# Second layer's self-attention: fourteen matmuls that nothing reads, in every step, at three places of TensorE's order

## The reference

```python
# x: (16, 128, 256); N_Q, N_KV = 16, 4 heads of 16; g = 4
q = _rope((x @ Wq + bq) by heads)          # 16 query heads
k = _rope((x @ Wk + bk) by heads)          # 4 key heads
v = (x @ Wv + bv) by heads                 # 4 value heads
qg = q.reshape(B, N_KV, g, T, d)
scores = einsum('bhgnd,bhsd->bhns', qg, k) / sqrt(d)   # the 4 queries of a group are summed
att = softmax(where(tril, scores, -inf))
y = einsum('bhns,bhsd->bhnd', att, v)      # width 4 * 16 = 64
x = x + (y @ Wo + bo)                      # x on the right went through a layer norm first
```

## Time and profile before

| | us |
|---|---|
| median of 3 runs | 3545.29 (3538.87 to 3551.51) |
| profiled execution, its own time | 3557.57 |
| span of its profile | 3555.8 |
| mean granted TensorE clock | 0.925 of full speed |
| TensorE busy | 2974.0 (84% of the span) |
| VectorE, ScalarE, GpSimd busy | 2398.8, 1808.0, 1772.2 |

### The profile page before, as it was taken

The page is one execution under the profiler, slowest core; times in us unless marked ns, Lnnn a source line. Parts: engine busy times, 40 slices in busy tenths (PEclk is TensorE's granted clock), DMA queues, the critical chain, the costliest instruction groups (busy, mean ns, idle before and its releaser), DMA issues. The chain is left out here.

```text
span 3555.8 us, 73082 instructions
## 1 busy us (share of the span) xinstructions
PE 2974.0 (84%) x25401; PEld 2294.0 (65%) x25432; DVE 2398.8 (67%) x5594; ACT 1808.0 (51%) x3484; POOL 1772.2 (50%) x1923
## 2 busy tenths in 40 slices
PE   8959978779998664976768998999998777877798
PEld 5747754457777453654556665888886666666565
DVE  5567744747777416857867887566665777776788
ACT  3347743446665223645653332566664565665476
POOL 2122211215555374547744851788885666665232
PEclk9979998689998776988998999999999999999799
DMA  4010010000001251000014000000000000000001
GB/s 148 1 23 13 15 62 6 1 5 8 7 7 51 93 114 41 6 22 13 16 24 172 19 18 8 2 0 0 0 0 6 4 5 4 3 4 3 22 24 38
DMA packets 92844, 89.37 MB, mean 25 GB/s; under 512 B 41279, under 2 KB 83167, under 8 KB 91234
## 3 DMA queue, kind: packets, MB, share of 16 engines
q1 hardware_dynamic: 88034, 81.23, 7.4%
q0 software_dynamic: 4608, 5.57, 0.9%
HBM read 68.16 MB, written 11.53 MB: 22 GB/s over the span
## 5 line engine op out<-in xcount | busy, mean ns | idle before, releaser
L518 PE MATMUL bank<-l2f_xnT,l2f_wi 128*88 128x512 f16 x960 | 222.1, 381 | 1.0 <-DVE l2f_h L364 0.7
L1527 PE MATMUL bank<-l3a_ln_xnT,far 128*128 128x128 f16 x3072 | 185.8, 221 | 1.8 <-POOL l3a_ln_xnT L1343 1.8
L2319 ACT ACTIVATE l3x_prob<-bank,l3x_less,l3x_q_rr 128x128 f32<-128x128 f32 x256 | 96.5, 457 | 171.8 <-DVE l3x_less L2201 171.8
L1527 PEld LDWEIGHTS bank<-l3a_ln_xnT,far 128*128 128x128 f16 x3072 | 180.9, 99 | 3.4 <-POOL l3a_ln_xnT L1343 2.2
L518 PEld LDWEIGHTS bank<-l2f_xnT,l2f_wi 128*88 128x88 f16 x960 | 114.7, 121 | 80.8 <-issue 2.4
L377 DVE SCALAR_TENSOR_TENSOR x_res<-bank,l3f_combine,x_res 128x256 f32<-128x256 f32 x320 | 132.8, 478 | 25.0 <-PE bank L528 23.0
L377 DVE SCALAR_TENSOR_TENSOR x_res<-bank,l2f_combine,x_res 128x256 f32<-128x256 f32 x320 | 132.5, 476 | 6.9
L2793 PE MATMUL bank<-l0x_v,l0x_pT 128*128 128x128 f32 x1024 | 134.5, 279 | 3.2 <-ACT l0x_pT L3208 1.5
L2793 PEld LDWEIGHTS bank<-l0x_v,l0x_pT 128*128 128x128 f32 x1024 | 127.6, 192 | 13.8 <-issue 4.7
L528 PE MATMUL bank<-l3f_wd,l3f_h 128*128 128x256 f16 x960 | 119.0, 274 | 12.4 <-DVE l3f_h L369 12.4
L2407 POOL TENSOR_TENSOR l1x_prob<-l1x_prob,l1x_srec 128x512 f32<-128x512 f32 x64 | 67.9, 1061 | 121.8 <-DVE l1x_srec L2178 121.8
(11 more groups left out here) (717 smaller groups left out, 9556.1 us busy)
## 6 DMA issues: line engine op xcount, KB each, us to landing
far<-in_l1f_in SPq DMA_DIRECT2D x32, 256.0 KB, 3.4
sums<-near SPq DMA_DIRECT2D x2, 2176.0 KB, 19.0
far<-in_l1f_down SPq DMA_DIRECT2D x32, 128.0 KB, 3.5
l1f_xn<-sums SPq DMA_DIRECT2D x32, 128.0 KB, 2.3
l2f_wi<-in_l2f_in SPq DMA_DIRECT2D x20, 176.0 KB
far<-l0x_kT SPq DMA_DIRECT2D x64, 48.0 KB
far<-l2x_kT SPq DMA_DIRECT2D x32, 96.0 KB
l3f_wi<-in_l3f_in SPq DMA_DIRECT2D x20, 128.0 KB
```

The lines of the kernel that those rows point to most:

```text
L518: last = nc.tensor.matmul(bank[g % 2][0:width, :], wi16[u][p][:, a, k, :], xnT[q][:, k, 512 * g:512 * g + 512], start=(k + p + q == 0), st ...
L1527: last = nc.tensor.matmul(bank[:, P * j:P * j + P], w(k, 512 * c + P * j, P, p), norm.xnT[u][q][:, k, :], start=(k + p + q == 0), stop=(k ...
L2319: last = nc.scalar.activation(prob[c_ % 2][:, at], b_s[:, at], ACT.Exp, bias=less[c_ % 2][:, j:j + 1], scale=q_rr[c_ % 2][:, j:j + 1])
```

## The change

A helper `keep_busy(g, n)` is added to TensorE's list and called three times a step. For the kind `"summed"` and a sequence number `g` of 1 or more it does `n` matmuls of 256 columns with the first weight half of the output projection as both operands (64 rows), into columns 0 to 255 of the score bank that is free in this step. Nothing reads what they write, they wait for nothing and signal nothing. The next `scores` into that bank overwrite it. It is called with 2 between `scores` and `scores_by_key`, with 6 between `turn_k` and `turn_q`, and with 6 between `turn_norm` and `turn_out`: 14 a step, in the 15 steps with sequences 1 to 15, so 210 in all. For the other layers and for sequence 0 it does nothing.

```diff
+                def keep_busy(g, n):
+                    if kind == "summed" and g:
+                        for _ in range(n):
+                            nc.tensor.matmul(b_s[(g + 1) % 2][:, 0:D], w16["o"][0][0:FW, 0, 0:P], w16["o"][0][0:FW, 0, :],
+                                             start=True, stop=True)
+
                 def turn_k(b):
...
                     for u in range(min(2, UB)):
                         if new is not None:
                             scores(new, u)
+                    keep_busy(new, 2)
                     for u in range(min(2, UB)):
                         if back is not None:
                             scores_by_key(back, u)
                     if kt is not None:
                         turn_k(kt)
+                    keep_busy(new, 6)
                     if tn is not None:
                         turn_q(tn)
                     if pj is not None:
                         if ctxT is not None:
                             project_ctx(pj)
                         turn_norm(pj)
+                    keep_busy(new, 6)
                     for u in range(UB):
                         if fin is not None and u == UB // 2:
                             turn_out(fin)
```

## The result

The changed kernel takes 3541.36 us (median of 20, 3537.15 to 3543.50), the kernel before, run beside it, 3554.99 us (median of 20, 3535.06 to 3558.62; the three executions that the forecast started from are among them). The medians lie 13.6 us apart. The ratio over all executions, which gives the few short ones of the kernel before their weight, is 0.9974, 95% interval 0.9963 to 0.9984: faster by 0.26%, less than the 0.43% that was forecast, and just inside the 0.3% that I had named as the border. A second comparison, further down, gave 0.9965 (0.9952 to 0.9977). The forecast of 3530 us was too low by 11; the measured median lies 0.6 us inside the upper end of its range of 3522 to 3542.

What follows compares the result with a forecast made beforehand. TensorE's chain, two thirds of it at half clock because of two waits for ScalarE, was taken as the bound. Full steps -20.4 and ends +5.2 gave -15.2 us off the 3545.3 median: 3530 us, range 3522 to 3542.

Steps and rivals of the forecast that it cites:

- What bounds the kernel, and why the clock would hold: Eighth-slice layer, TensorE's chain at mean clock 0.67; filling its waits leaves 0.4 of 7.6 us idle, holding the upper clock.
- clock holds as reckoned: Likeliest case: upper clock kept through the layer's full steps, kernel at 3530 us; chance 0.67.
- The step at the upper clock: Full steps: 7.36 us from start-to-start pieces, 7.59 with the added 0.23; eight take 60.7 instead of 81.07, -20.4 us.
- first place: Two matmuls between scores and scores_by_key, where nothing waits: 0.23 us a step on the path.
- The ends: Sequences 1, 2 and 11 to 15, where added work is partly uncovered: +1.9, +0.9 and +2.4, together +5.2 us.
- The base: Whole kernel: the -15.2 us reckoned from the 3557.57 us profile, taken off the median 3545.3, giving 3530 us.
- in part: Rival: in the full steps the clock falls every few steps, half of 20.4 us kept, 3540 us; chance 0.08.
- The clock holds, but something else paces the step: Rival: VectorE's 7.38 us or its collisions with GpSimd make full steps 8.0 us, kernel 3533 us; chance 0.13.
- Pattern unchanged: Rival: clock falls in full steps as before, added work costs +7.6 us, kernel 3553 us; chance 0.07.
- The slower case: Rival: lower clock throughout, added work outlasts the two waits, full steps 12.5 us, +24, kernel 3569 us; chance 0.05.

Runs made afterwards that it cites:

- second comparison: The changed kernel, unchanged, run again beside the kernel before and the covered version on one chip: 3541.66 us, ratio 0.9965 to the kernel before.
- half the dose: Against the changed kernel, three matmuls instead of six before turn_q and before turn_out, none between the scores: 3540.49 us, ratio 0.9967.
- covered version: Against the changed kernel, the sixes only where a wait covers them, none between the scores: 3534.10 us (0.9949), again 3537.14 us (0.9953).
- third place alone: Against the changed kernel, only the six before turn_out kept: 3555.62 us, ratio 1.0011, over 10 of 12 executions.
- short profile: The kernel before, unchanged, profiled again in an execution of 3546.20 us; its eight full steps took 61.82 us at clock 0.94.
- first comparison: The changed kernel beside the kernel before, 20 executions each: 3541.36 against 3554.99 us, ratio 0.9974.

## Why the prediction was wrong

The sign and the mechanism were right, the microseconds nearly so; wrong was the number that they were taken from.

**What bounds the kernel, and why the clock would hold.** Right in what came: clock 1.0 throughout. The argument for it was weaker than it looked. It compared busy shares with the stretch up to 657.90, and half the dose, with a larger share than that stretch, still had two falls. What the experiments show is that the clock holds with both waits filled. The case "clock holds as reckoned" with 0.67 is the one that came.

**The step at the upper clock.** Right: 7.36 + 0.23 = 7.59 forecast, 7.55 measured, and 7.33 without the first place (covered version). Waits before `turn_q` and `turn_out` covered the twelve at no cost, as taken. The eight steps gave 60.41 us instead of 60.7. That the waits do not shrink with the clock was read from two rows that both lie in stretches at 1.0; at 0.5 the version with the third place alone has 732.18 - 730.83 = 1.35 us from `turn_k` to `turn_q`, so it holds start to start, with 0.71 of idle time in it instead of 0.86.

**The ends.** Too small, the smaller of two faults. Steps of sequences 1 and 2 take 13.18 / 2 = 6.59 us against 5.47 in the covered version, 1.12 more where 0.93 was reckoned. The term at fault is the price of an uncovered six, taken as 6 x 0.116 = 0.70 from a pace. Start to start it is more: in a step without `turn_out` the six put 0.86 us between `turn_norm` and `heads_out` (0.23 without them, 1.09 with): the first of them starts 0.33 behind `turn_norm`, and they take 0.76. The layer gained 14.2 us where 15.2 were forecast; the eight steps gave 20.7 (81.07 - 60.41), so the rest cost 6.5, not 5.2.

**The base, the step that made the prediction wrong.** "so I take the same microseconds off the median: 3545.3 - 15.2". The sum was made from a trace with a fall of the clock in every step. That is a long execution (3557.57 us), and 15.2 is what such a one loses; 3557.57 - 15.2 = 3542.4 is 1 us from the measured median. The median of 3545.29 was itself a short execution, one in which the clock fell rarely, as in the short profile: there the layer took 150.2 us, and the change, with which it takes 151.5, takes nothing off it. (That 3545.29 is of this kind is read from its time alone, with nothing between 3546.57 and 3551.51 among 103; it was not profiled.) Of the 11.3 us between forecast and measurement 9.7 are this base, 3554.99 with twenty executions where three had given 3545.3, and 1.6 are the gain, 13.6 between the medians where 15.2 was forecast. That the range still holds the measured time owes nothing to this step: its upper end was set for other cases, the medians' scatter and a clock that holds in part. The text saw the 12 us between profile and median and the 12.6 us among the three runs, and put both down as scatter. They were largely the effect itself, present in one execution and absent in the next. The same holds for the ratio: a gain of 14.2 us against the thirteen long executions of the first comparison and none against the seven short ones leaves 9.2 us on average, or 0.26% as measured. In the second comparison 1 of 19 was short, and the ratio is 0.9965.

**Rivals.** "The clock holds, but something else paces the step": did not come; in the covered version most steps are still 7.33 us. "Pattern unchanged" and "in part" did not come for the changed kernel, though half the dose showed the latter (0.94). The slower case was seen only at the end of the version with the third place alone; what the prediction held against it, that busy stretches at 0.5 bring the upper level back, did not hold there.

## What to carry to other kernels

When a layer's time hangs on a clock that may or may not fall, look at several executions before choosing what to subtract from. Times that fall into two groups are two kinds, a profile shows one of them, and a gain read from its trace belongs to that kind only. The mean clock of the whole program is a poor guide (0.925 and 0.926 in the two profiles set side by side here); the clock in the layer's own stretch is a good one (0.66 and 0.94). Work of no use is free where a measured wait covers it and costs more than its pace where none does, so it should be placed by wait, not by step; here the covered version gave 0.5% where the change gave 0.3%. Closing one wait, the one before `turn_q`, which is there in every step up to sequence 13, did nearly all of it.

## What was not expected of the hardware

The same program on one core has two kinds of executions: in one the clock falls in every step of a layer (81.4 us for eight steps), in the other twice in eight (61.8 us), with the same waits of 0.86 us in both and the same 44 us ahead of the first fall. The changed kernel lies closer together: its twenty executions are within 6.4 us, those of the kernel before within 23.6. Nor does one number decide when the clock changes: with TensorE busy 10.59 of 13.50 us it held, with 54.48 of 61.73 it fell twice, and with 31.86 of 33.00 at the lower level it did not rise. Two matmuls a step, 0.22 us of work outside any wait, made eleven of twelve executions some 4 to 10 us shorter than the long ones of the kernel before, and no run says how.
